# Layer 1 of a graph network: the spherical attributes as six row groups, one product of 96 rows per 128 edges, three transfers per tile

## What is computed

```python
h = silu(edge_attr @ fc1 + b1); h = silu(h @ fc2 + b2)
scale = h @ fc3 + b3
msg = silu(x_src @ W_node * scale + edge_sh @ W_sh)      # edge_sh: 16 numbers per edge
a = silu(concat([x_src[:, :64], x_dst[:, :64], edge_attr]) @ aW1 + ab1)
a = silu(a @ aW2 + ab2) @ aW3 + ab3
alpha_mean = softmax(a, axis=0).mean(axis=1)
agg = segment_sum(msg * alpha_mean, dst)
out = layernorm(node_features + agg @ W_out)
```

## Time and profile before

| | us |
|---|---|
| median of 3 runs | 4765.45 |
| lowest and highest | 4763.96, 4783.84 |
| the profiled execution, whole | 4772.5 |
| its span, first to last instruction | 4770.6 |
| layer 0's edge loop, first to last load issue | 409.8 to 2109.6 |
| layer 1's edge loop, first to last load issue | 2385.9 to 4135.4 |

### The profile page before, as it was taken

How to read it: one execution, slowest core, us unless ns; L and a number is a source line. 1 busy time by engine, 2 the same in 40 slices (tenths; PEclk the granted TensorE clock), 3 DMA queues, 4 the chain that set the end, 5 groups by cost and what they waited for, 6 DMA issues and landing times. The chain is left out here.

```text
span 4770.6 us, 78804 instructions
## 1 busy us (share of the span) xinstructions
PE 3193.8 (67%) x16644; PEld 2002.4 (42%) x16868; DVE 2941.9 (62%) x5753; ACT 1708.5 (36%) x3040; POOL 2200.2 (46%) x2274
## 2 busy tenths in 40 slices
PE   0024666666666666661489999999999999836664
PEld 0012444545455454540144444444444444435553
DVE  6576877778777877889733333333333333477776
ACT  0411444444444444440144444444444444410001
POOL 0004666666666766750155555555555555400001
PEclk9567888888888888885899999999999999979997
DMA  1934343334333433430355555666656566524552
GB/s 57 332 136 123 113 113 112 106 112 114 110 111 110 118 110 114 118 91 2 109 167 177 173 177 176 175 173 177 176 176 176 175 175 175 155 79 147 146 147 63
DMA packets 440626, 655.46 MB, mean 137 GB/s; under 512 B 81381, under 2 KB 294943, under 8 KB 440578
## 3 DMA queue, kind: packets, MB, share of 16 engines
q1 hardware_dynamic: 305410, 319.26, 23.3%
q0 software_dynamic: 98304, 268.57, 19.3%
q10 hardware_dynamic: 36864, 67.13, 3.7%
HBM read 530.01 MB, written 124.50 MB: 137 GB/s over the span
## 5 line engine op out<-in xcount | busy, mean ns | idle before, releaser
L662 POOL DMA_INDIRECT l_G<-rows_d,l_sidx x1024 | 1163.6, 1136 | 523.4 <-issue 299.9
L1059 POOL DMA_INDIRECT l_G<-rows_d,l_sidx x1024 | 972.2, 949 | 799.1 <-ACT l_h L1198 319.8
L686 PE MATMUL l_A<-ident,l_G 128*128 128x128 f32 x1024 | 196.6, 323 | 612.9 <-DVE l_oht L820 457.1
L1267 DVE TENSOR_SCALAR l_oht<-l_lo,mine_bc 128x512 bf16<-128x512 bf16 x256 | 95.9, 375 | 792.2 <-DMA l_sh<-sh_d 713.3
L1198 ACT ACTIVATE l_h<-l_H,l_cols 128x512 f32<-128x512 f32 x512 | 349.2, 682 | 487.3 <-remote 280.3
L730 PE MATMUL l_accp<-l_we,l_ohe 128*128 128x256 f32 x2048 | 521.6, 401 | 0.0
L1397 PE MATMUL ag_accp<-ag_msg,ag_pick 128*128 128x128 f32 x2048 | 303.6, 294 | 215.3 <-DVE ag_pick L1441 210.6
L686 PEld LDWEIGHTS l_A<-ident,l_G 128*128 128x128 f32 x1024 | 127.1, 160 | 712.3 <-issue 424.8
L730 PEld LDWEIGHTS l_accp<-l_we,l_ohe 128*128 128x128 f32 x2048 | 402.6, 208 | 49.8
L1397 PEld LDWEIGHTS ag_accp<-ag_msg,ag_pick 128*128 128x128 f32 x2048 | 256.7, 197 | 262.4 <-DVE ag_pick L1441 160.1
L758 ACT ACTIVATE l_e<-l_A 128x512 f32<-128x512 f32 x256 | 153.0, 597 | 586.4 <-remote 354.8
(11 more groups left out here) (187 smaller groups left out, 6416.6 us busy)
## 6 DMA issues: line engine op xcount, KB each, us to landing
msg_d<-l_msg ACTq DMA_DIRECT2D x256, 256.0 KB
ag_msg<-msg_d SPq DMA_DIRECT2D x256, 256.0 KB, 2.6
l_G<-rows_d,l_sidx POOLq DMA_INDIRECT x2048
l_lo<-mark_d SPq DMA_DIRECT2D x256, 128.0 KB
l_lo<-code_d SPq DMA_DIRECT2D x256, 128.0 KB
l_fd<-dst_d SPq DMA_DIRECT2D x256, 96.0 KB
l_pd<-dst_d SPq DMA_DIRECT2D x256, 96.0 KB
l_ea<-ea_d SPq DMA_DIRECT2D x256, 96.0 KB
```

The costliest lines, as they stand in the source:

```text
L662: nc.gpsimd.indirect_dma_start(out=G[:, s, j, :], out_offset=None, in_=rows_d[0][:, :], in_offset=bass.IndirectOffsetOnAxis(ap=sidx[:, hal ...
L686: nc.tensor.matmul(av[:, j, :], G[:, s, j, 0:C], ident[:, :], is_transpose=True, start=(j == 0), stop=False, skip_group_check=True)
L1059: nc.gpsimd.indirect_dma_start(out=G[:, s, j, :], out_offset=None, in_=rows_d[1][:, :], in_offset=bass.IndirectOffsetOnAxis(ap=sidx[:, hal ...
```

## The change

`sh_t` gets 96 rows instead of 64: the groups x0, x1, x2, x0, x1, x0. `w_sh_t` becomes one block of 96 rows, w0, w0, w0, w1, w1, w2. One product of 96 rows per group of 128 edges takes the place of the two, so four products per item instead of eight. The tile is loaded by three transfers, of 48, 32 and 16 rows, instead of two, so SP issues seven transfers per item, and the waits on `ld[s]` count 112 instead of 96. `ea_t` and its weights stay as they are. In the setup `w_sh_t` is still placed by six transfers.

```diff
--- before.py
+++ after.py
@@ -926,7 +926,7 @@
                 lo_t = sb("l1_lo", [P, U, IT], BF16, st)
                 pd_t = sb("l1_pd", [P, U, 3 * C], BF16, st)
                 ea_t = sb("l1_ea", [4 * EA, U, IT], BF16, st)
-                sh_t = sb("l1_sh", [4 * SH, U, IT], BF16, st)
+                sh_t = sb("l1_sh", [6 * SH, U, IT], BF16, st)
                 oht = sb("l1_oht", [P, R, IT], BF16, st)
                 h1_t = sb("l1_h1", [P, 2, IT], F32, st)
                 a1_t = sb("l1_a1", [P, 2, IT], F32, st)
@@ -939,7 +939,7 @@
 
                 w_fc1 = sb("l1_fc1", [4 * EA, 2, C], BF16, st)
                 w_aw1 = sb("l1_aw1", [4 * EA, 2, C], BF16, st)
-                w_sh_t = sb("l1_wsh", [4 * SH, 2, C], BF16, st)
+                w_sh_t = sb("l1_wsh", [6 * SH, 1, C], BF16, st)
                 small = [big[0:EA, k * C:(k + 1) * C] for k in range(3)]
                 small_rest = big[0:EA, 3 * C:4 * C]
                 small_cut = [big[0:EA, (8 + 3 * k) * C // 2:(11 + 3 * k) * C // 2].bitcast(BF16).rearrange(
@@ -1006,7 +1006,7 @@
                                          ab3.rearrange("(p k) -> p k", k=1)).then_inc(s_w, 16)
                         sp.wait_ge(s_cut, CUTS)
                         for k, (t, n) in enumerate(((w_fc1, EA), (w_aw1, EA), (w_sh_t, SH))):
-                            for half, parts in enumerate(((0, 0, 0), (1, 1, None, 2))):
+                            for half, parts in enumerate(((0, 0, 0), (1, 1, None, 2)) if n == EA else ((0, 0, 0, 1, 1, 2),)):
                                 for group, m in enumerate(parts):
                                     if m is not None:
                                         sp.dma_start(t[group * n:(group + 1) * n, half, :],
@@ -1027,7 +1027,10 @@
                             sp.dma_start(pd_t[:, s, :], dst_d[1][bass.ds(row, P), :]).then_inc(ld[s], 16)
                             for t, d, n in ((ea_t, ea_d, EA), (sh_t, sh_d, SH)):
                                 sp.dma_start(t[0:3 * n, s, :], d[:, bass.ds(off, IT)]).then_inc(ld[s], 16)
-                                sp.dma_start(t[3 * n:4 * n, s, :], d[0:n, bass.ds(off, IT)]).then_inc(ld[s], 16)
+                                if n == EA:
+                                    sp.dma_start(t[3 * n:4 * n, s, :], d[0:n, bass.ds(off, IT)]).then_inc(ld[s], 16)
+                            sp.dma_start(sh_t[3 * SH:5 * SH, s, :], sh_d[0:2 * SH, bass.ds(off, IT)]).then_inc(ld[s], 16)
+                            sp.dma_start(sh_t[5 * SH:6 * SH, s, :], sh_d[0:SH, bass.ds(off, IT)]).then_inc(ld[s], 16)
 
                         def step(lap, u):
                             rows(lap, u, 0)
@@ -1073,7 +1076,7 @@
                             if not exists(i, NI):
                                 return
                             g, _ = ring(s, lp)
-                            pe.wait_ge(ld[s], 96 * (lp + 1))
+                            pe.wait_ge(ld[s], 112 * (lp + 1))
                             if after(i, 1):
                                 pe.wait_ge(h1s, i)
                             nc.tensor.matmul(H1[:, :], w_fc1[0:3 * EA, 0, :], ea_t[0:3 * EA, s, :], start=True, stop=False)
@@ -1128,8 +1131,7 @@
                             if after(i, 1):
                                 pe.wait_ge(pre_ready, i)
                             for j in range(TJ):
-                                nc.tensor.matmul(SP_[:, j, :], sv[0:3 * SH, j, :], w_sh_t[0:3 * SH, 0, :], start=True, stop=False)
-                                last = nc.tensor.matmul(SP_[:, j, :], sv[:, j, :], w_sh_t[:, 1, :], start=False, stop=True)
+                                last = nc.tensor.matmul(SP_[:, j, :], sv[:, j, :], w_sh_t[:, 0, :], start=True, stop=True)
                             last.then_inc(sh_ready, 1)
 
                         def back(lap, u, d):
@@ -1261,7 +1263,7 @@
                             if not exists(i, NI):
                                 return
                             g, _ = ring(s, lp)
-                            dve.wait_ge(ld[s], 96 * (lp + 1))
+                            dve.wait_ge(ld[s], 112 * (lp + 1))
                             if after(i, R):
                                 dve.wait_ge(a1p, i - R + 1)
                             nc.vector.tensor_scalar(oht[:, g, :], lo_t[:, s, :], mine_bc[:, bass.ds(i, 1)], None,
```

## The result

| first comparison | us |
|---|---|
| before, median of 5 | 4771.04 (4763.96 to 4783.84) |
| after, median of 5 | 4819.24 (4807.91 to 4830.23) |
| ratio | 1.0098, 95% interval 1.007 to 1.0125 |
| the profiled execution of after | 4830.23, span 4828.4 |

The change costs 48 us, 1.0%. The forecast was 133 us, and its range began at 4824.

A forecast was written before the change was run, and what follows sets the result against it. SP's load queue was taken to bound layer 1. Profiled 4772.5 us + 133 for the seventh issue - 0 for the products = 4905.5; with the median 7.05 us lower, the forecast was 4898 us, 2.8% slower, range 4824 to 4965.

The forecast's parts named there:

- What bounds the kernel: Layer 1's edge stage: SP's load queue, never held, is the slowest stage at 6.86 us an item; TensorE waits for it.
- The seventh issue: SP in layer 1: one more transfer issue per item costs 0.52 us, times 256 items 133 us.
- rival C: SP's long steps absorb the added issue, the item shortens elsewhere by as much: 4765 us, up to 24 more; chance 0.08.
- the half-way value of 0.23: Lower bound of the seventh issue's price: half of the undisturbed 0.46 us vanishes, leaving 0.23 us an item, 4824 us.
- The upper bound, 0.78 us,: Seventh issue's highest price, if SP's long steps come per unit of its time: 0.78 us an item, 4965 us.
- TensorE's 0.24 us: Layer 1's four products fewer save 0.24 us an item, 61 us in all, valued at nothing because TensorE waits for SP.
- Rival B: TensorE bounds layer 1 after all, the new issue is hidden and 61 us go: 4704 us; chance 0.06.
- Clock, landing, waits: TensorE's granted clock, the 32 KB more per item landing, and the waits for 112: each put at nothing.
- some 130: Expected sign in the profile: VectorE's one-hot waits some 130 us longer for `l_sh`.

The follow-up runs named there:

- x3r: Kernel before with two of the four gathers per item in layer 1, run where SP's steps were long: 4575.8 us beside 4768.1, ratio 0.9588.
- the pads: Four more SP register loads per item: on the kernel before 4451.8 us, with a seventh transfer too 4543.4, on the change 4547.1; unpadded before 4219.3.
- the quiet sets: Sets of runs without SP's long steps, the kernel before near 4216 us; there the change took 4101.6 us beside 4216.7, ratio 0.9724.
- x2r_one_product: Kernel before with the change's single 96-row product but six transfers, run with long SP steps: 4703.8 us beside 4714.1, ratio 0.9974.
- the parts: With long SP steps, kernel before plus only the seventh transfer: ratio 1.0073, 34 us more; with only the 96-row products: ratio 0.9974, 12 us less.
- v_act_loads: The change's products with six transfers, sh_d stored as four parts, SP waiting less, sh_t's two loads on ACT's queue: 4112.6 us beside before's 4215.1, ratio 0.976.
- b_before: Kernel before, unchanged, run once for its profile in a set without long SP steps: 4218.8 us.

## Why the prediction was wrong

**What bounds the kernel: right for its trace.** That SP's queue, not TensorE, set layer 1's pace was read from the missing holds, and x3r and the pads confirm it: take the long steps away and SP is held again; make SP slow by even steps and TensorE's products stop counting (4 us of 4547). With long steps they still gave 12 us.

**The seventh issue: the term that failed.** The step "I take 0.52" took the distance from one issue to the next for the price of an issue. The slot was right, 0.48 us measured. But the price is what the whole item becomes longer, and that was 0.20 us, since the other slots shrank by 0.30. A bound SP with even steps paid 0.36 to 0.38, one with long steps 34, 48, 53 and 198 / 3 us, or 0.13 to 0.26 us an item (the 48 and 53 have the halved products in them). That is rival C's mechanism, at about half strength; I had given it full absorption or none, and the half-way value of 0.23 only as the bound of the range, which the measured 0.19 to 0.20 us passed. The trace of before held a hint that I didn't weigh: over items 20 to 239, those whose issue part was 1 us longer had a remainder 0.45 us shorter on average. Whether this is the absorption itself was not shown.

**The upper bound, 0.78 us,** supposed that long steps come per unit of SP's time. The count fell from 3.3 to 2.6 an item with more time in the item, so they don't.

**TensorE's 0.24 us: mis-sized too.** It came from the spacing inside the group, and that part was right (0.25 us). The sentence that 96 rows instead of 48 or 64 cost nothing left out that they give something: TensorE saves 0.45 us (period 6.08 to 5.63), since the entry into the group and the exit from it shrink by 0.09 us each. In the first comparison the error cost nothing, as the term was valued at nothing.

**Rival B: wrong here, right elsewhere.** "An SP with spare time would run ahead until it is held" is what the quiet sets show, and there B's direction holds with nearly twice its price, 115 us instead of 61. I gave B 0.06 on one trace of one condition; the runs of before that I had all lay at 4764 to 4784 us and gave no sign of another. The Trainium skill's sentence that starting a DMA is usually small relative to the DMA itself (DMA: Bandwidth & Descriptors, "Issuing engines are not separate DMA queues") would have given the sign that the quiet sets have; with long SP steps the measurement decides against it. So does the padded SP, where an issue costs 0.36 us; in the quiet sets it is free because TensorE is the bound.

**Clock, landing, waits:** as forecast of no effect on the pace. VectorE's wait for the loads grew by 273 us, not by some 130: it is slack beside the bound, and part of it came from other waits: the idle time before L1289 (L1291 after) fell from 184 to 8 us. The granted clock in layer 1 was 0.98 before and 0.99 after.

**Open.** What makes the long steps come and go between sets of runs with the same program. How a gather reaches SP's sequencer; that the steps need about the density of four gathers an item is shown for this kernel only. What absorbs part of an added issue, with long steps and, by 0.10 us, without. Why x2r_one_product gains 12 us, and why the parts sum up to 22 us where the change costs 53. And whether v_act_loads holds its gain under long steps.

## What to carry to other kernels

A queue that is never held, while other engines wait for what it issues, is the bound, and the list of its own waits shows it in one line; but the price of one more instruction on it is the change of the whole period, to be measured, not the length of its slot. When register steps of one line spread from 18 to 700 ns, the balance between engines rests on something outside the program: work out the edit for the quiet case as well, and expect that its sign may differ. Where a small issue can go to a queue with spare time, as in v_act_loads, the issuing queue gets slack back (478 us of 1300 there); what that is worth while it is the bound was not measured.

## What was not expected of the hardware

One program ran at 4215 us and at 4768 us, both repeatable within a set to about 1%, and the traces differ in SP's instruction steps of about 0.7 us in the stages in which GpSimd gathers: 3.3 an item with four gathers, 0.5 with two, and no register step of 0.2 us or more in the stages without. The queues of ScalarE, GpSimd and VectorE have no such register steps in the layer 1 of the same trace (none in 946, 421 and 737, against 405 in 3645 on SP). Of the 554 us between b_before and the first before (4216.9 and 4770.6), 348 lie in layer 0's loop (first to last load 411.8 to 1763.7 against 409.8 to 2109.6), where SP was held for 510 us and so didn't look like a bound; the longer time goes with the long steps there as well, by what path was not examined. The granted clock of layer 0 was 0.85 in the one and 0.96 in the other, and VectorE, busy for 96% of the loop in b_before, was busy for 78% of it. Products of 96 rows by 128 columns start 0.055 to 0.058 us apart, and those of 48 and 64 rows nearly as close, 0.058 to 0.067; but a group of the latter between products of 128 rows costs 0.18 us an item more at its two ends.
